# First attention of a two-layer network: raw rows for two tiles, later key turns, wider score products

## The reference, cut to what matters

```python
def _L0_xattn_ref(text, features, Wq_w, Wq_b, Wk_w, Wk_b, fn_w, qn_w, kn_w):
    features_n = rmsnorm(features, fn_w)
    Q = einsum('btd,fd->btf', text, Wq_w) + Wq_b
    K = einsum('bsd,fd->bsf', features_n, Wk_w) + Wk_b
    Q, K = rmsnorm(Q, qn_w), rmsnorm(K, kn_w)
    scores = einsum('btf,bsf->bts', Q, K) / sqrt(512)
    attended = einsum('bts,bsf->btf', softmax(scores), features_n)

x = x + _L0_xattn_ref(_layernorm(x), ctx_4096, ...)
x = x + _L0_ffn_ref(_layernorm(x), ...)
x = x + _L1_xattn_ref(_layernorm(x), ctx_4096, mask, ...)
x = x + _L1_ffn_ref(_layernorm(x), ...)
```

## Time and profile before

| | |
|---|---|
| median of 3 runs | 1510.65 us |
| the profiled execution | 1511.27 us |
| its span, first to last instruction | 1509.5 us |
| mean granted TensorE clock | 0.994 of full |
| TensorE, VectorE busy | 1463.2, 1127.8 us |
| ScalarE, GpSimd busy | 795.1, 710.3 us |

### The profile page before, as it was taken

How to read it: one execution, slowest core, us unless ns; L and a number is a source line. 1 busy time by engine, 2 the same in 40 slices (tenths; PEclk the granted TensorE clock), 3 DMA queues, 4 the chain that set the end, 5 groups by cost and what they waited for, 6 DMA issues and landing times.

```text
span 1509.5 us, 27579 instructions
## 1 busy us (share of the span) xinstructions
PE 1463.2 (97%) x9895; PEld 846.4 (56%) x9895; DVE 1127.8 (75%) x2172; ACT 795.1 (53%) x3201; POOL 710.3 (47%) x668
## 2 busy tenths in 40 slices
PE   5999999999999799999999999999999999999998
PEld 4888745555555455555555555555565555555554
DVE  5788787878876888776776676677677677667868
ACT  5678841211223576556546654754664565565763
POOL 5668875454565353334334343433434333343553
PEclk9999999999999999999999999999999999999999
DMA  7454435333344565653553554455445445334622
GB/s 248 147 175 136 123 81 126 98 77 50 65 88 72 117 147 84 110 119 64 100 105 53 95 88 81 86 87 95 81 80 105 79 73 103 64 60 67 99 50 112
DMA packets 358936, 146.87 MB, mean 97 GB/s; under 512 B 342304, under 2 KB 342688, under 8 KB 356112
## 3 DMA queue, kind: packets, MB, share of 16 engines
q1 hardware_dynamic: 357504, 137.77, 45.1%
q10 hardware_dynamic: 1296, 7.34, 1.5%
HBM read 58.02 MB, written 4.19 MB: 41 GB/s over the span
## 4 chain that ended last, share of the span: by engine, by line
PE 55%; DVE 5%; ACT 3%; DMA 1%; POOL 1%; issue 1%; SPq 0%; DVEq 0%; POOLq 0%; ACTq 0%
PE bank L72 18%; PE bank L74 17%; PE bank L73 17%; PE bank L2439 3%; ACT a_prob L1836 2%; DMA a_pT_lo<-a_p_lo 1%; POOL a_prob L1707 1%; DVE a_oT_lo L2106 1%; DVE x_res L2193 1%; DVE a_qve L2045 1%; ACT a_oT_lo L1813 0%; DVE a_p_lo L2094 0%; DVE a_nmx L2082 0%; DVE a_qr_lo L2035 0%; POOL a_xr_lo L1731 0%
## 5 line engine op out<-in xcount | busy, mean ns | idle before, releaser
L1836 ACT ACTIVATE a_prob<-a_prob,a_nmx 128x64 f32<-128x64 f32 x512 | 170.2, 334 | 183.7 <-DVE a_nmx L2082 183.7
L72 PE MATMUL bank<-w,a_oT_hi 128*128 128x512 f16 x512 | 194.0, 379 | 1.8 <-DVE a_oT_lo L2106 0.9
L74 PE MATMUL bank<-w,a_oT_hi 128*128 128x512 f16 x512 | 194.0, 379 | 0.0
L73 PE MATMUL bank<-w,a_oT_lo 128*128 128x512 f16 x512 | 194.0, 379 | 0.0
L72 PE MATMUL bank<-w,xT_hi 128*128 128x448 f16 (+1 forms) x512 | 188.0, 367 | 3.1 <-DVE h L1231 2.0
L73 PE MATMUL bank<-w,xT_lo 128*128 128x448 f16 (+1 forms) x512 | 187.7, 367 | 0.0
L74 PE MATMUL bank<-w,xT_hi 128*128 128x448 f16 (+1 forms) x512 | 187.5, 366 | 0.0
L1707 POOL TENSOR_TENSOR a_prob<-a_prob,a_mask 128x512 f32<-128x512 f32 x64 | 79.8, 1268 | 204.5 <-DVE a_prob L2076 204.5
L2031 DVE SCALAR_TENSOR_TENSOR x_res<-bank,a_oinv,x_res 128x512 f32<-128x512 f32 x128 | 95.5, 746 | 75.0 <-PE bank L74 75.0
L1157 ACT CAST f_h_hi<-h 128x448 f16<-128x448 f32 x64 | 35.6, 563 | 209.7 <-DVE h L1231 209.6
L1719 POOL TENSOR_TENSOR a_krs<-a_kve,neg_half 128x4 f32<-128x4 f32 x32 | 32.8, 1026 | 239.6 <-DVE a_kve L2056 239.6
(11 more groups left out here) (351 smaller groups left out, 4120.5 us busy)
## 6 DMA issues: line engine op xcount, KB each, us to landing
shared<-in_l_wq SPq DMA_DIRECT2D x8, 1024.0 KB, 5.0
shared<-in_l_wo SPq DMA_DIRECT2D x8, 1024.0 KB, 5.1
shared<-in_w ACTq DMA_DIRECT2D x8, 896.0 KB, 4.7
craw<-in_w SPq DMA_DIRECT2D x11, 512.0 KB, 3.9
...
```

The source lines that it names most:

```text
L72: pe.matmul(out, a_hi, b_hi, start=first, stop=False)
L73: pe.matmul(out, a_lo, b_hi, start=False, stop=False)
L74: return pe.matmul(out, a_hi, b_lo, start=False, stop=last)
L1836: ins = act.activation(pt, pt, ACT.Exp, bias=nmx[:, col:col + 1], accum_out=den[:, col:col + 1])
```

## The change

It touches the first attention, and one place in the FFN's filler work.

- Rows of tiles 0 and 1 (`RAW = 2`) are not normalised before the projection. They are loaded turned from memory (`l0_xT`), ScalarE rounds them and GpSimd takes the rest. The mean is taken out of the query weights instead: GpSimd and VectorE add the four blocks of `l0_wq`, TensorE multiplies by 1/512 (`thin`) into `w_mean`, VectorE subtracts it from each block before the split. The row's root is applied in the query bias of these tiles.
- TensorE turns keys of tile n behind the key projection of tile n+1, and the probabilities of tile n-1 behind that. Attend(n-1) comes before `rows_T(n+2)`.
- Scores: per block two products of 256 columns, query hi and query lo, each against key hi and key lo side by side (`kT_both`). The two halves of the result are added by VectorE in a second step. Per tile 8 products instead of 12; lo x lo is now in.
- GpSimd takes `features_lo(n)` and `weigh(n+1)` first in its body, behind its wait for scaled keys. `weigh(0)` waits for all split weights.
- The w1 maxima stand in tiles 2 to 5, statistics for the FFN in 4 to 7, its normalisation and turns one tile earlier. VectorE, ScalarE and SyncE are reordered to match.

```diff
-    xT4_hi, xT4_lo = (big[:, (4 + h) * KD * D:(5 + h) * KD * D].rearrange("p (k f) -> p k f", k=KD) for h in range(2))
+    turned = big[:, 4 * KD * D:6 * KD * D].rearrange("p (k f) -> p k f", k=KD)
+    kT_both = turned[:, :, 6 * P:8 * P]
-    MAX_AT = {n: n - 1 for n in range(1, 5)}
+    MAX_AT = {n: n - 2 for n in range(2, 6)}
-    STAT_AT = {5 + t: t for t in range(TPC)}
+    STAT_AT = {4 + t: t for t in range(TPC)}
# GpSimd
+        def add_wq(out, half):
+            pool.wait_ge(wq_in[half], 16)
+            pool.tensor_tensor(out, w_raw[0][:, 2 * half, :], w_raw[0][:, 2 * half + 1, :], ALU.add).then_inc(s_mean, 1)
+        def rows_T(n):
+            pool.wait_ge(s_xTh, n + 1)
+            pool.tensor_tensor(xT_lo[:, :, :], xT_raw[n][:, :, :], xT_hi[:, :, :], ALU.subtract).then_inc(s_xTl, 1)
         def body(n, first=False, ahead=True, project=True):
-            tile_roots(n)
+            if first:
+                tile_roots(n)
+            features_lo(n)
+            if project:
+                weigh(n + 1)
+            if not first:
+                tile_roots(n)
             if ahead:
                 features_T(n + 2)
             if project:
                 key_root(n + 1)
                 pool.wait_ge(s_kn, n + 2)
# ScalarE, body
+            if n and project:
+                rows_T(n + 1)
+            q_T(n)
...
+            if n != NT - 1:
+                k_T(n)
+            if not first:
+                probs_T(n - 1)
+            if project:
+                key_squares(n + 1)
+            if ahead:
                 normalise(n + 2)
# VectorE, body
-            dve.wait_ge(s_nmx, n * 2 + 1)
+            dve.wait_ge(s_nmx, n * 3 + 1)
+            dve.scalar_tensor_tensor(prob[:, :], b_s[:, P:2 * P], qrs(n), prob[:, :], ALU.mult, ALU.add).then_inc(s_nmx, 1)
+        def centre_wq(k):
+            dve.tensor_tensor(w_raw[0][:, k, :], w_raw[0][:, k, :], w_mean[:, :], ALU.subtract).then_inc(s_mean, 1)
# TensorE, body
             if project and not first:
+                pe.wait_ge(s_kb, n + 1)
                 project_k(n + 1)
+            if n != NT - 1:
+                k_T(n)
+            if not first:
+                probs_T(n - 1)
+            if project:
                 project_q(n + 1)
             for k in range(KD):
-                ins = split_mm(pe, b_s[:, 0:P], qT_hi[:, k, :], qT_lo[:, k, :], kT_hi[:, k, :], kT_lo[:, k, :],
-                               k == 0, k == KD - 1)
+                pe.matmul(b_both, qT_hi[:, k, :], kT_both[:, k, :], start=k == 0, stop=False)
+                ins = pe.matmul(b_both, qT_lo[:, k, :], kT_both[:, k, :], start=False, stop=k == KD - 1)
             ins.then_inc(s_s, 1)
+            if n == NT - 2:
+                k_T(n + 1)
+                q_T(n + 1)
+            if not first:
+                attend(n - 1)
             if ahead:
                 rows_T(n + 2)
-            if not first:
-                attend(n - 1)
-            if project:
                 q_T(n + 1)
-                k_T(n + 1)
# TensorE, before the first body
         project_k(0, first=True)
-        rows_T(0)
-        project_q(0, first=True)
+        pe.wait_ge(s_mean, 3)
+        pe.matmul(w_mean[:, :], thin[:, :], w_sum, start=True, stop=True).then_inc(s_mean, 1)
         pe.wait_ge(s_kb, 1)
         project_k(1)
+        project_q(0, first=True)
         q_T(0)
-        k_T(0)
-        rows_T(1)
```

391 lines of the change are left out of this document (215 added, 176 removed).

## The result

The changed kernel took 1514.18 us (median of 20 runs, 1511.28 to 1518.24), the kernel before beside it 1510.57 (20 runs). The ratio is 1.0026 [1.0019, 1.0032]: slower by 3.9 us, where 5.5 less was forecast. The same kernel in a later comparison gave 1.0031 [1.0018, 1.0043]. The profiled execution took 1513.16 us.

The account below looks back on a forecast made before the run. TensorE sets the pace, VectorE close behind. Terms -5.6 - 3.5 + 0 + 0.5 + 3.0 + 0.9 + 0.5 - 1.3 = -5.5 took the profiled 1511.27 us to 1505.8, 1505.2 as a median; range for 8 in 10: 1500 to 1511.

Parts of the forecast that it names:

- Scores: TensorE's score products: eight of 256 columns at 0.120 us replace twelve of 128, 0.37 less per tile, -5.6 us.
- These 3.5 us go: TensorE's key turn, moved behind the next key projection, no longer waits for VectorE's scaled keys: -3.5 us.
- VectorE's backlog: VectorE, with a second score step and side work, falls behind; TensorE waits in tiles 5, 6 and 8: +3.0 us.
- Tiles 10 to 13: VectorE's loop through the FFN turns and row split sums to 9.3 us, 0.3 more a tile: +0.9 us.
- w2 scales before the key turn of tile 14: VectorE's w2 scales stand ahead of tile 14's key turn: +0.5 us.
- The last tile: The old score wait of 1.4 us goes, a new one of 1.4 for split queries and keys comes: 0.
- The start: Up to tile 2's projection, which was to begin at 35.6 instead of 36.90 us: -1.3 us.
- the mean's product: TensorE's fp32 product forming the query weights' mean in the start: 1.7 us taken, between 0.23 and above 2.
- every other new wait: Key projection for key bias, key bias for scaled keys, query bias for squares: each on something half a tile old, 0.
- Rival 1: In the attention tiles VectorE keeps the gain and TensorE waits for it in every tile: 1510.6 us, chance 0.20.
- rival 4: The start gets longer: the mean arrives behind the key projection, query weights 3 us later, +6, 1511 us; chance 0.07.
- the rival of products that don't overlap: In the scores, weight load and stream of 256-column fp32r products do not overlap: 1518.8 us, chance 0.08.

Follow-up runs that it names:

- both repairs: Also written a_lc: changed kernel, ScalarE issuing the last two w1 loads one tile earlier and its low-rank-factor copies moved within tile 6; 1508.70 us, 0.9982 to the kernel before.
- a_lc_vh: On top of both repairs, VectorE takes the w2 maxima over only half of each piece, leaving work out; 1508.11 us, 0.9987 to the kernel before.
- a_lcw2b: On top of both repairs, w2 maxima one tile later, their turn in another bank behind attend of tile 13, scales ending VectorE's tile 14; 1508.40 us, 0.9984.

## Why the prediction was wrong

- Scores, 0.120 a product: right (0.119). -5.6 for 15 tiles: wrong. The 0.37 was seen in tile 2 and, in part of the executions, in tile 3, where TensorE sets the pace. The steps of 0.12 were never the doubt; whether TensorE is the bound in each of the 15 tiles was.
- "These 3.5 us go": this step failed too. The waits of the key turn ended by name, since the turn moved, but what had made the scaled keys late stayed: GpSimd's tile with the FFN's root (10.36 before, 10.31 after, 9.4 to 9.5 with its w1 split halved in either kernel) and tiles with side work on VectorE. Before, 5.8 us of the stage lay above 13 tiles of 8.93. I booked part of them as gone and took the whole score saving on top. With both repairs TensorE still idles 8.8 us in the stage.
- VectorE's backlog, +3.0 in tiles 5, 6 and 8: right in kind, too small. With both repairs tiles 5, 6 and 8 lie 1.43, 1.78 and 1.27 over 8.58, where I had 1.5, 1.05 and 0.45. Tile 6 holds the scales and a w2 maximum. I took 1.2 us for the scales from the earlier trace rows; from 85.72 to 87.80 they took 2.08, 0.87 of it in the operation that stood beside GpSimd's. Halving the maximum gave 0.75 there, with that operation back at 0.17, and 0.44 in tile 8.
- Tiles 10 to 13, "9.0 to 9.3": 9.4 to 9.5 and, in 13, 10.4 with both repairs. I named VectorE's loop, with a sum of 9.3 that no row was given for; a_lc_vh shows that its w2 maximum is not in the bound. The chain read above runs through ScalarE and GpSimd. The surplus of tile 13 goes with the copy beside GpSimd's weighing.
- w2 scales before the key turn of tile 14, +0.5: unresolved. With them moved away, together with the maxima and their turn (a_lcw2b), tiles 13 and 14 took 0.49 less and the last tile 0.71 more.
- The last tile, 0: from the last query turn to the low-rank product are 10.77 before and 10.36 after, but that turn stands earlier in the new order, so this term stays unresolved.
- The start, -1.3: the projection of tile 2 began at 35.48 (35.6 forecast), and the third query turn at 45.31 against 47.31. Right within the scatter. The terms as I listed them add up to 35.45, not 35.6, and the mean's product, taken as 1.7 us, took 1.13. TensorE's timeline, answering:

```profile
35.07 0.66 PE L903 MATMUL bank<-ident,a_wide 128*128 128x128 f32 x4 [3.02 <-DVE a_wide L688]
35.48 0.49 PE L72 MATMUL bank<-a_big 128*128 128x512 f32 x1
```

- Not in the sum at all: ScalarE. This is the step that decided the sign. Behind the priced waits I put "every other new wait" at 0 and listed three, none of them ScalarE's. Its block of the low-rank factors ahead of the copy of the turned rows, and its w1 scaling ahead of the key copy, together 4.4 us of the stage. It is the largest missing term: without it the change is faster by 2.7 us (a_lc), half of the 5.5 that were forecast.

The stage of the first profile missed by 9.8 (138.25 to 128.4): 4.2 by ScalarE's two positions (138.25 to 134.04; 4.4 on the mean of both profiles), and 5.6 by the first two steps and the too small backlog, which these runs don't split further. No rival named ScalarE. Rival 1 (VectorE keeps the gain, 1510.6) comes nearest in what happened, since it also covered waits that only change their name, but its 1510.6 lacks the costliest part; rival 4 (a longer start, 1511) is the nearest number and is refuted, since the start got shorter; the rival of products that don't overlap (1518.8) is refuted by the step of 0.119.
